# Constants built by ACT and by transfers instead of POOL, small weights and gate rows moved, the first block's silu taken tile by tile

## The reference, cut to what matters

```
mod = (silu(c) @ wmod).reshape(8, 6, 1, -1)           # shift, scale and gate, twice
ga = (2 * (ga >= 0) - 1) * maximum(abs(ga), 0.25)     # the same for gb
h = layernorm(x) * (1 + ca) + sa
xn = layernorm(h, ln_w, ln_b)
z, xBC, dt = split(xn @ in_proj_w)
dt = softplus(dt + dt_bias);  xBC = silu(causal_conv1d(xBC, conv_w, conv_b))
A = -exp(A_log)
y = ssd_scan(x_ssm, dt, Bm, Cm, A) + D_skip * x_ssm   # state decays by exp(dt * A)
y = y * silu(z);  y = y * rsqrt(mean(y**2) + eps) * rms_w
out = y @ out_proj_w + h                              # then an MLP with relu, residual
x = x + ga * (MLP output);  x = x + gb * feed_forward(layernorm(x) * (1 + cb) + sb)
```

## Time and profile before

| | us |
|---|---|
| median of 3 runs (2977.11 to 2982.07) | 2977.18 |
| the profiled execution's own time | 2984.3 |
| its span in the trace | 2982.6 |
| from the span's start to PE's first transpose of block 0 | 32.62 |
| from there to the first tap on DVE | 20.81 |
| from there to the first exponential of `mh` | 29.10 |

### The profile page before, as it was taken

The page is one execution under the profiler, slowest core; times in us unless marked ns, Lnnn a source line. Parts: engine busy times, 40 slices in busy tenths (PEclk is TensorE's granted clock), DMA queues, the critical chain, the costliest instruction groups (busy, mean ns, idle before and its releaser), DMA issues. The chain is left out here.

```text
span 2982.6 us, 46128 instructions
## 1 busy us (share of the span) xinstructions
PE 2751.3 (92%) x17002; PEld 2069.1 (69%) x17002; DVE 1787.5 (60%) x3232; ACT 1395.2 (47%) x2400; POOL 636.2 (21%) x717
## 2 busy tenths in 40 slices
PE   4899999999998996999997999999999999999999
PEld 2455555555555553888886878878787887878787
DVE  6898999999999985677763332333333323333332
ACT  3877777777777773555652222222222222222221
POOL 4122222222222222000001222222222122222221
PEclk7899999999999998999998999999999999999999
DMA  2111011101010111431220000000000000000000
GB/s 65 40 50 37 22 38 28 38 23 37 22 37 22 37 30 63 142 138 66 68 72 24 15 17 1 15 17 15 17 15 17 15 1 17 15 17 15 17 15 8
DMA packets 104137, 100.51 MB, mean 34 GB/s; under 512 B 35816, under 2 KB 98536, under 8 KB 103024
## 3 DMA queue, kind: packets, MB, share of 16 engines
q1 hardware_dynamic: 102320, 97.41, 10.4%
q10 hardware_dynamic: 1600, 0.04, 0.0%
HBM read 69.05 MB, written 38.85 MB: 36 GB/s over the span
## 5 line engine op out<-in xcount | busy, mean ns | idle before, releaser
L1691 PE MATMUL fbank<-hid,fw 128*128 128x512 f32 x4096 | 962.3, 395 | 0.0
L1691 PEld LDWEIGHTS fbank<-hid,fw 128*128 128x128 f32 x4096 | 766.2, 187 | 186.9
L1841 DVE TENSOR_TENSOR hid<-fhf,hid 128x512 fp32r<-128x512 f32 x384 | 265.0, 690 | 704.9 <-POOL hid L1798 704.9
L1798 POOL TENSOR_SCALAR hid<-fhf 128x512 fp32r<-128x512 f32 x384 | 271.0, 706 | 1051.1 <-ACT fhf L1770 761.4
L1198 DVE SCALAR_TENSOR_TENSOR mh<-mh,gm 128x1024 f32<-128x1024 f32 x256 | 353.6, 1387 | 0.0
L915 ACT ACTIVATE mh<-ebank 128x512 f32<-128x512 f32 x512 | 294.7, 597 | 107.1 <-PE ebank L762 104.5
L1770 ACT ACTIVATE fhf<-fbank,sh2c 128x512 f32<-128x512 f32 x128 | 88.0, 688 | 382.4 <-PE fbank L1691 382.4
L762 PE MATMUL ebank<-cright,cleft 102*128 102x512 bf16 x512 | 210.5, 412 | 58.4 <-ACT mh L915 53.6
L775 PE MATMUL yin<-mh,xpad 128*32 128x128 f32 x4096 | 228.5, 297 | 28.3 <-DVE mh L1198 28.2
L749 PE MATMUL ebank<-ah,win 128*128 128x512 f32 x640 | 247.6, 430 | 5.2 <-ACT cin L948 5.2
L1770 ACT ACTIVATE fhf<-fbank,sh1c 128x512 f32<-128x512 f32 x128 | 88.1, 688 | 320.8 <-PE fbank L1691 320.6
(11 more groups left out here) (185 smaller groups left out, 4291.9 us busy)
## 6 DMA issues: line engine op xcount, KB each, us to landing
fx<-x_d SPq DMA_DIRECT2D x17, 512.0 KB, 3.9
xs<-in_x SPq DMA_DIRECT2D x16, 512.0 KB, 4.2
h_d<-in_h SPq DMA_DIRECT2D x16, 512.0 KB, 5.1
o_d<-o SPq DMA_DIRECT2D x16, 512.0 KB, 2.8
mo<-o_d SPq DMA_DIRECT2D x16, 512.0 KB, 3.8
mx<-in_x SPq DMA_DIRECT2D x16, 512.0 KB, 4.8
x_d<-mx SPq DMA_DIRECT2D x16, 512.0 KB, 2.8
fw<-h_d SPq DMA_DIRECT2D x2, 4096.0 KB, 15.3
```

Of the source, the lines that this page charges most:

```text
L1691: mm = pe.matmul(bank[banks.slot(key)][:], w[:, k, m * P:(m + 1) * P].bitcast(dt), h[:, k, :].bitcast(dt), start=(k + n == 0), stop=(k == ...
L1798: pool.tensor_scalar(hid[i % 2][0][:, m, :], hf[j % 3][:], 1.0, 0.0, ALU.mult, ALU.add)\
L1841: dve.tensor_tensor(hid[i % 2][1][:, m, :], hf[j % 3][:], hid[i % 2][0][:, m, :].bitcast(F32), ALU.subtract).then_inc(c_lo.sem, 1)
```

## The change

The constants: `sel` and a small tensor `crow` (6x128 values that matter, one row for each of the last rows) are made first by POOL; ACT copies `sel` into rows 0 to 95 of both `cright`, and SP sends `crow` into rows 99 to 101 with two transfers. POOL makes the rest (`ident`, `tri`), takes the first norm's power, makes `cleft` and `pick`, and takes the second norm's power, all in the first block. `normalise(0, 1)` stands in ACT's first block. The semaphores' start values are added by PE and not by SP. The wait for the small vectors moves from the end of the first block (SP and ACT) to the head of ACT's second. `nega` and the scaling of `wout` are done by ACT behind block 0's softplus (`small_weights`), `mag` by ACT behind the second `affine`, the gate rows by DVE behind the second `low`, and the store of `mod_d` by SP in the second block. Block 0's silu goes tile by tile, `xc` first and `sz` behind it (`first_gates`); POOL's first product with `sz` gets a wait of its own.

```
         @block.sync
         def _(sp):
-            start(sp, counts)
...
             sp.dma_start(wout[:], g["w_out"].rearrange("(k p) n -> p k n", p=P)).then_inc(s_wout, 16)
-            sp.wait_ge(s_modrow, 3)
-            sp.dma_start(mod_d, mod[:].rearrange("b i j d -> b (i j d)")).then_inc(s_store, 16)
-            sp.wait_ge(s_vec, 16 * vecs)
-            sp.wait_ge(s_store, 16)
+            sp.wait_ge(s_made, 2)
+            for r in range(2):
+                sp.dma_start(cright[r][99:LEFT, :, :], crow[99:LEFT, :].unsqueeze(1).to_broadcast([LEFT - 99, NH, P]))\
+                    .then_inc(s_right, 16)
...
             nc.scalar.activation(ct[:], ct[:], ACT.Silu).then_inc(s_silu, 1)
+            act.wait_ge(s_made, 1)
+            nc.scalar.activation(cright[0][0:96, :, :], sel[:].unsqueeze(2).to_broadcast([96, NH, P]), ACT.Copy)
             act_normalise(act, 0, 0)
-            act.wait_ge(s_vec, 16 * vecs)
-            nc.scalar.activation(nega[:], nega[:], ACT.Exp).then_inc(s_a, 1)
-            act.wait_ge(s_mod, 1)
-            nc.scalar.activation(mod[:], mp[:], ACT.Copy).then_inc(s_modrow, 1)
-            act.wait_ge(s_modrow, 1)
-            nc.scalar.activation(mag[:], mod[:, :, 2, :], ACT.Abs, scale=2.0).then_inc(s_mag, 1)
+            nc.scalar.activation(cright[1][0:96, :, :], sel[:].unsqueeze(2).to_broadcast([96, NH, P]), ACT.Copy)
             for k in range(KD):
                 act.wait_ge(s_stage[k], 16)
                 nc.scalar.activation(win[0][:, k, :], stage[:, k, :], ACT.Copy).then_inc(s_high, 1)
+            act_normalise(act, 0, 1)
+            act.wait_ge(s_mod, 1)
+            nc.scalar.activation(mod[:], mp[:], ACT.Copy).then_inc(s_modrow, 1)
 
         @block.tensor
         def _(pe):
+            start(pe, counts)
...
+            pool_power(pool, 1)
             for j in range(2):
+                in_turn(pool.memset(cleft[j][:], 1.0))
                 v = cleft[j][96:LEFT, :, :]
+                in_turn(pool.affine_select(out=v, in_=v, compare_op=ALU.is_ge, fill=0.0,
+                                           base=(LEFT - 96 - 4) * STRIP, pattern=[[0, NC], [1, P]],
+                                           channel_multiplier=-STRIP))
             pool.sem_inc(s_fill, 1)
+            in_turn(pool.tensor_scalar(pick[:].rearrange("k q (h d) -> k (q h) d", d=HD),
+                                       sel[:].unsqueeze(2).to_broadcast([96, NH, HD]), -1.0, 0.0, ALU.mult, ALU.add))
+            pool_power(pool, 2)
...
+            def first_gates():
+                for m in range(XM):
+                    act.wait_ge(c_conv.sem, c_conv.at(0, m + 1))
+                    ins = nc.scalar.activation(xc[0][:, m, :], xc[0][:, m, :], ACT.Silu)
+                ins.then_inc(c_xc.sem, 1)
+                released(act, ("in", 0, QI - 1))
+                nc.scalar.activation(sz[0][:], sz[0][:], ACT.Silu).then_inc(s_z, 1)
...
-            normalise(0, 1)
+            def small_weights():
+                nc.scalar.activation(nega[:], nega[:], ACT.Exp).then_inc(s_a, 1)
+                act.wait_ge(s_wout, 16)
+                for f in range(QI):
+                    nc.scalar.activation(wout[:, f, :], wout[:, f, :], ACT.Copy, scale=rmsw[:, f:f + 1])
+                act.wait_ge(s_a, 1)
+                nc.scalar.activation(nega[:], nega[:], ACT.Copy, scale=-1.0).then_inc(s_a, 1)
+
+            act.wait_ge(s_vec, 16 * vecs)
...
-            pool_power(pool, 2)
-            for r in range(2):
-                pool.sem_inc(s_fill, 1)
-                pool.tensor_copy(cright[r][0:96, :, :], sel[:].unsqueeze(2).to_broadcast([96, NH, P]))                    .then_inc(s_zero, 1)
...
-                pool.memset(v, 0.0).then_inc(s_zero, 1)
...
-                pool.affine_select(out=v, in_=v, compare_op=ALU.is_ge, fill=NEVER, base=(LEFT - 96 - 4) * STRIP,
-                                   pattern=[[0, NH], [1, P]], channel_multiplier=-STRIP).then_inc(s_zero, 1)
...
-            for f in range(QI):
-                pool.tensor_scalar(wout[:, f, :], wout[:, f, :], rmsw[:, f:f + 1], None, ALU.mult)
```

More of the change, by code:

```diff
@@ L445, in mixer @@
     sel = sb("sel", [96, NH], BF16)
+    crow = sb("crow", [LEFT, P], BF16)
+    mod = sb("mod", [B, 2, 3, D])
+    mag = sb("mag", [B, 2, D])
+    sign = sb("sign", [B, 2, D])
+    s_vec, s_store, s_modrow = sem("s_vec"), sem("s_store"), sem("s_modrow")
+    s_mag, s_sign, s_a = sem("s_gate_size"), sem("s_gate_sign"), sem("s_a")
     with ExitStack() as own:
@@ L559, in _ @@
             layer_norms(0, 3)
[L560 to L566, removed]
@@ L577, in _ @@
-            pool.memset(tri[:], 1.0)
-            pool.memset(sel[:], 0.0)
-            for j in range(2):
[L580 to L583, removed]
-                               pattern=[[-1, P]], channel_multiplier=1)
-            pool.affine_select(out=tri[:], in_=tri[:], compare_op=ALU.is_ge, fill=0.0, base=0,
-                               pattern=[[1, P]], channel_multiplier=-1).then_inc(s_made, 1)
@@ L587, in _ @@
-            pool.wait_ge(s_made, 2)
-            for j in range(2):
-                v = cleft[j][96:LEFT, :, :]
-                last = pool.affine_select(out=v, in_=v, compare_op=ALU.is_ge, fill=0.0,
-                                          base=(LEFT - 96 - 4) * STRIP, pattern=[[0, NC], [1, P]],
-                                          channel_multiplier=-STRIP)
-            last.then_inc(s_made, 1)
-            pool.wait_ge(s_made, 3)
-            for j in range(3):
-                pool.affine_select(out=sel[:], in_=sel[:], compare_op=ALU.not_equal, fill=-1.0, base=-NH * j,
-                                   pattern=[[-1, NH]], channel_multiplier=1).then_inc(s_made, 1)
-                pool.wait_ge(s_made, 4 + j)
+            done = [0]
@@ new lines, in in_turn @@
+            def in_turn(ins):
+                done[0] += 1
+                ins.then_inc(s_turn, 1)
+                pool.wait_ge(s_turn, done[0])
+            in_turn(pool.memset(sel[:], 0.0))
+            for j in range(3):
+                in_turn(pool.affine_select(out=sel[:], in_=sel[:], compare_op=ALU.not_equal, fill=-1.0, base=-NH * j,
+                                           pattern=[[-1, NH]], channel_multiplier=1))
+            pool.sem_inc(s_made, 1)
+            v = crow[96:LEFT, :]
@@ L705, in _ @@
                 sp.wait_ge(c_norm.sem, c_norm.at(0, j + 1))
+                if j == 1:
+                    sp.wait_ge(s_store, 16)
                 load(j + 1)
                 if j == 0:
+                    sp.wait_ge(s_modrow, 3)
+                    sp.dma_start(mod_d, mod[:].rearrange("b i j d -> b (i j d)")).then_inc(s_store, 16)
+                    sp.wait_ge(s_right, 32)
                     decay_left(0)
-                    sp.wait_ge(s_right, 2)
                     decay_right(0)
@@ L1029, in _ @@
                         affine(j, AFFINE_AT.index(n))
+                    if S == FIRST + AFFINE_AT[1]:
+                        nc.scalar.activation(mag[:], mod[:, :, 2, :], ACT.Abs, scale=2.0).then_inc(s_mag, 1)
                     if n == SOFTPLUS_AT:
                         softplus(j)
+                    if S == FIRST + SOFTPLUS_AT:
+                        small_weights()
                     if n in EVAC_AT:
@@ L1139, in chain, with gate_rows @@
                     dve.tensor_copy(p_[:, 2, :], crest[:, 1, :]).then_inc(c_cum.sem, 1)
+            def gate_rows():
+                dve.tensor_scalar(mod[:, :, 1, :], mod[:, :, 1, :], 1.0, None, ALU.add).then_inc(s_modrow, 1)
+                dve.tensor_scalar(sign[:], mod[:, :, 2, :], 0.0, 0.5, ALU.is_ge, ALU.subtract).then_inc(s_sign, 1)
+                dve.wait_ge(s_sign, 1)
+                dve.wait_ge(s_mag, 1)
+                dve.scalar_tensor_tensor(out=mod[:, :, 2, :], in0=mag[:], scalar=0.5, in1=sign[:], op0=ALU.max,
+                                         op1=ALU.mult).then_inc(s_modrow, 1)
             def weights(j):
```

53 lines of the change are left out of this document (22 added, 31 removed).

## The result

| | before | changed |
|---|---|---|
| median on the same chip, us | 2978.43 (2977.11 to 2982.07, 4 runs) | 2957.28 (2956.14 to 2958.43, 4 runs) |
| profiled execution: own time / span, us | 2984.3 / 2982.6 | 2956.14 / 2954.4 |

The ratio is 0.9922 (0.9908 to 0.9935), a gain of 23 us (19 to 27); the medians lie 21.15 us apart and the two traces 28.2 us.

The account below looks back on a forecast made before the run. The time of the first exponential of `mh`, 82.53 us, was taken to count, with DVE bounding the steady mixer behind it. 9.8 + 9.6 - 0.5 = 18.9 us off 2977.2 gave 2958.3, range 2951 to 2966.

Parts of the forecast that it names:

- part 1: First block, to PE's first transpose: earlier transfers and no wait of POOL's power for the border, gain 9.8 us.
- part 2: Front of block 0, first transpose to first tap: DVE's series no longer stands behind POOL's passes, gain 9.6 us.
- part 3: First tap to first exponential of `mh`: silu in six pieces and new order, a loss of 0.5 us.
- PE's own first product needs weights that are a transfer behind, so it hides them: First block: PE's wait for its weights covers the start values moved there from SP, priced at 3.0 us.
- moves up by 3.0: First block: everything hanging on the tokens' transfer comes 3.0 us earlier, the variance from 19.2 to 16.2.
- upper bound of this part: Part 1's gain if nothing holds DVE or POOL, given as 11.5 us.
- T: Time of PE's first transpose, 32.62 us before, from which part 2 counts.
- PE did not keep its high clock: Rival at z's products: the clock stays up across the shorter gap, gain 21.4 us, 2955.8; chance 0.15.
- the case that they don't: Rival in the first block: transfers don't start earlier, part 1 gives 6.8 us or less, 2961 to 2965; chance 0.12.
- the sign of being wrong: Prediction wrong if PE's transposes start after 26 us; they were expected at 22 to 23.5.
- No steady part got slower: Rival in the mixer's 64 chunks: POOL's gate products hold DVE more often; 0.5 us each would give 2990; chance 0.03.
- Nothing behind the front changes: Mixer's steady part and later phases: not tied to absolute time, so an earlier start ends them equally earlier.

Follow-up runs that it names:

- nothing but 49 increments: Kernel before with 49 more increments of a semaphore nobody waits for, on PE behind its last product of the first block: 2973.06 us, ratio 0.9965.
- mended kernel: Changed kernel with start values on SP behind six transfers, 49 idle PE increments, `mod` copied before the second norm, DVE waiting for `nmean`: 2951.17 us, ratio 0.9901.
- idle passes of POOL: Changed kernel with six POOL passes of the old sizes, which nothing needs, at the head of POOL's second block: 2967.65 us (one run).
- the kernel with 196 increments: Changed kernel with start values on SP behind six transfers and 196 idle increments on PE behind its last product of the first block: 2973.95 us.
- 24 to 98 increments: Kernels with that many more PE increments than before; changed kernel with start values on SP behind six transfers: 2949.16 us with 24, 2955.73 with 98.

## Why the prediction was right or wrong

| term | forecast | by the traces |
|---|---|---|
| part 1, to PE's first transpose | 9.8 | 6.7 (32.62 to 25.90) |
| part 2, from there to the first tap | 9.6 | 10.3 (20.81 to 10.53) |
| part 3, from there to `mh` | -0.5 | +0.75 (29.10 to 28.35) |
| front | 18.9 | 17.75 |
| mixer and MLP | 0 | 0.4 |
| feed-forward loop | 0 | 9.7 (8.1 with nothing but 49 increments) |

**Part 1: the step that failed** is "PE's own first product needs weights that are a transfer behind, so it hides them". It does not: PE's weights landed at 7.6 and its product starts at 8.49, behind the increments. And the semaphores of the others get their start values there too, so DVE's statistics waited for the last of them. I priced 49 increments at the 3.0 us that SP takes; PE takes 7.3. The statistics start at 8.17 instead of 5.4: 2.0 us for the start values, and 0.8 because the tokens' transfer itself takes 4.9 us instead of 4.1, so that "moves up by 3.0" was wrong too. `cleft` and `pick` cost 0.2 of the 0.7 that I had given them (statistics to variance 10.98 us, before 10.77), which puts the variance at 19.15 instead of 16.9. The rest of the miss is POOL's power and product beside DVE's `win`: from the variance to ACT's norm it took 2.89 us (19.15 to 22.04) where the forecast had 2.04. 2.25 + 0.85 = 3.1, which is all of 25.90 - 22.8. The norm (2.07), `mod` (1.42) and the border came as forecast. The mended kernel's 22.56 shows that 22.8 was to be had, but not as forecast: its variance is at 17.72, and it gains the rest by hiding `mod` and by keeping DVE off POOL's power. (By its own terms the upper bound of this part is 9.8 + 0.7 + 0.6 = 11.1, not 11.5.)

**Part 2** held in its mechanism and nearly in size. The series begins at T + 7.50 (forecast 7.4), takes 3.0 us to the tap (3.2), and the table load costs its 1.28 with 0.01 us behind it, so no drain shows here either. `wout`'s scaling took 1.69 us, and the first tile and its `cin` were ready at 35.82 and 36.30, ahead of the series' end: the tap did not wait for ACT as I had said, which is the 0.7 us that part 2 gained over its term. The idle passes of POOL confirm the mechanism from the other side.

**Part 3** had the wrong sign and a small size. The six pieces of silu took 3.23 us (forecast 3.6), and taking them whole changes nothing. The 0.75 us gained lies in DVE's first steps behind the first tap: from it to the scan `cum`, before took 5.32 us (53.43 to 58.75) with POOL's four `wout` passes beside it for 4.6 of them, and the changed kernel, without them, takes 4.59 (36.43 to 41.02). No run put those passes back alone.

**The rivals.** PE did not keep its high clock for z's products, though it now waited 3.56 us ahead of them instead of 15.76 before:

```profile
46.76 0.48 PE L863 MATMUL ebank<-ident,dtv 128*128 128x128 f32 x1 [3.56 <-DVE wv L1157]
```

Two stretches of the changed kernel (length, PE's busy time and count, PE clock, DMA share, GB/s), the convolution tiles and the time steps' and z's products:

```profile
36.00:43.20 7.20, 7.20 (x31) 1.00 0.02 5
46.76:52.40 5.64, 5.64 (x16) 0.50 0.07 13
```

The granted clock is 0.50 in the second, the same 1.2 GHz as in the earlier trace rows, after 7.20 us without a gap at 1.00 and a wait of 3.56. The transfers left early, but part 1 still fell just short of the 6.8 I gave for the case that they don't, and the transposes at 25.90 lie 0.1 us inside the 26 that I had named as the sign of being wrong. No steady part got slower: the mixer took 1074.99 us for 1075.13.

**Nothing behind the front changes** was the larger error: I looked for semaphores' waits that tie the rest to the front, found none, and held the rest for fixed. What moved is where PE's later instructions lie. Of the 23 us (19 to 27) measured, the forecast's mechanisms explain 17.75, the loop 8 to 10; that the median came within about 1 us of 2958.3 is luck: two misses of opposite sign and the spread of the runs. Between executions the mixer alone took 1066.7 to 1075.3 us in fourteen traces, 1074.99 and 1069.95 in two of the same changed kernel, so a difference of single spans such as 28.2 is not known to better than some 5 us.

**Open:** what ends the pause at the seventh product, and why the kernel with 196 increments brings its instructions in again without having one; why 24 to 98 increments keep them and 0 and 196 do not (where the loop lies in its blocks of 16 KB would fit, which is not shown); and why the change to start values on PE alone measured 15 us where its trace shows 8.7 in front and loop. That one pause per pass stays in the kernels without such transfers is the wait for `gb`; with 196 increments PE is 1.5 to 2.0 us late at its first product and has hardly any of it left (0.24 us, once). No run loads `gb` earlier, which should give most of the remaining 10 us (an estimate, from the pauses' total).

## What to carry to other kernels

Price semaphore increments by the engine that makes them, and ask whose semaphores get them: a wait of the issuing engine covers only its own. A POOL pass over a large constant can cost DVE its whole length even when nobody needs it yet, so build constants on an engine that waits or by a transfer. When an edit changes the number of instructions on PE ahead of a loop, compare the loop's own time, the duration of its branch and the instruction queue's packets too: 49 idle increments were worth as much as one of the planned parts. And look at what stands behind a pause that goes away: here half of the gain was taken back by a transfer that had been late all along.

## What the runs showed of the hardware that was not expected

- PE takes 0.15 us for a semaphore increment (49 from 0.9 to 8.2 us), SP 0.06 (49 in the 3.0 us before its first transfer at 3.81).
- A kernel becomes 10 us faster by 49 increments without effect: the loop's instruction packets fall from 53 to none, and PE's branch back to its head from 3.35 us to 0.21.
- POOL is slowed by DVE as DVE is by POOL: the power of 128x4 takes 1.03 us alone and 2.12 beside `win`.
- Not every POOL pass holds every DVE instruction. In the four traces with the six passes, DVE's `TENSOR_SCALAR` stood beside the memset and the affine_select (up to 4.06 us); its instructions with two tensor inputs stood beside the copy and the affine_select (up to 3.99 us) but not beside the memset, which reads nothing: `dsq` takes its 0.29 us at 45.56 in the kernel before, and `al` its 0.69 at 35.24 and 36.58. The reciprocal was held by none.
